# Two attention phases rearranged: transposes one tile later in the second, steps of two key tiles in the first

## The reference

```python
# first attention (layer 0), 16 heads of 16; the last 16 context rows have an attention of their own
q = _ln((x @ Wq + bq).reshape(b, s1, H, HD), qn_w, qn_b)
k = _ln(kv[..., :HD], kn_w, kn_b);  v = kv[..., HD:]        # 1484 rows
s = jnp.einsum('bhqd,bhkd->bhqk', q, k) * SCALE
p = jax.nn.softmax(s, axis=-1)
ctx = jnp.einsum('bhqk,bhkd->bhqd', p, v)
# second attention (layer 1), 16 heads of 128, 1500 rows
q = rmsnorm(q, gq);  k = rmsnorm(k, gk)
scores = jnp.einsum('bqhd,bkhd->bhqk', q, k) * scale
out = jnp.einsum('bhqk,bkhd->bqhd', jax.nn.softmax(scores, axis=-1), v)
```

## Time and profile before

| what | value |
|---|---|
| median of 3 runs | 2623.57 us (2622.91 to 2623.58) |
| the profiled execution, its own time | 2625.33 us |
| its span, first to last instruction | 2623.6 us |
| mean granted TensorE clock | 0.903 of full speed |
| PE busy | 2223.8 us (85%) |
| DVE, ACT, POOL busy | 1781.6, 1187.0, 1236.7 us |
| first attention, first scores to the end of its last products | 913.05 to 1392.5 us |
| second attention, first scores to the last batch's maxima | 1724.17 to 2415.0 us |

### The profile page before, as it was taken

The page is one execution under the profiler, slowest core; times in us unless marked ns, Lnnn a source line. Parts: engine busy times, 40 slices in busy tenths (PEclk is TensorE's granted clock), DMA queues, the critical chain, the costliest instruction groups (busy, mean ns, idle before and its releaser), DMA issues. The chain is left out here.

```text
span 2623.6 us, 47067 instructions
## 1 busy us (share of the span) xinstructions
PE 2223.8 (85%) x16760; PEld 1749.7 (67%) x16760; DVE 1781.6 (68%) x2275; ACT 1187.0 (45%) x2007; POOL 1236.7 (47%) x988
## 2 busy tenths in 40 slices
PE   6999999999954599999996776958898989898675
PEld 4887888787832476666674343448888888888543
DVE  5878888888855465555552336968888888887057
ACT  5888888888820154445451123513232323233202
POOL 5666666666510243333330211318686868687300
PEclk9999999999976599999998687979898989899887
DMA  3232323232213133222220622241121212120500
GB/s 99 111 143 109 142 109 142 109 139 113 120 54 86 69 117 113 103 105 103 103 77 31 205 80 75 86 121 50 50 98 49 98 49 98 49 99 20 208 5 14
DMA packets 93876, 246.16 MB, mean 94 GB/s; under 512 B 19409, under 2 KB 65394, under 8 KB 84450
## 3 DMA queue, kind: packets, MB, share of 16 engines
q1 hardware_dynamic: 87602, 231.17, 24.6%
q10 hardware_dynamic: 4608, 9.44, 0.9%
q0 software_dynamic: 1536, 3.67, 0.5%
HBM read 144.25 MB, written 100.01 MB: 93 GB/s over the span
## 5 line engine op out<-in xcount | busy, mean ns | idle before, releaser
L1150 POOL TENSOR_TENSOR a_S<-a_S,a_mb 128x896 f32<-128x896 f32 x192 | 523.2, 2762 | 218.3 <-ACT a_mb L1173 218.3
L317 DVE TENSOR_REDUCE rk<-n_sq 128x1024 f32 (+2 forms) x384 | 465.6, 1213 | 129.3 <-ACT n_sq L255 126.9
L255 ACT ACTIVATE n_sq<-n_slot 128x1024 f32<-128x1024 f32 (+1 forms) x384 | 394.3, 1027 | 140.3 <-PE n_slot L211 131.8
L994 PEld LDWEIGHTS a_ob<-a_y,a_S 128*128 128x128 f32 (+1 forms) x2688 | 346.8, 203 | 6.9 <-issue 1.9
L994 PE MATMUL a_ob<-a_y,a_S 128*128 128x129 f32 (+1 forms) x2688 | 349.8, 286 | 1.7 <-issue 1.7
L209 PE MATMUL n_slot<-n_wh,n_yh 128*128 128x512 f32 (+1 forms) x768 | 318.3, 414 | 25.1 <-POOL n_yl L153 25.1
L1453 DVE TENSOR_REDUCE a_mpart<-a_pre 112x2 f32<-112x1024 f32 (+1 forms) x192 | 219.1, 1178 | 176.1 <-PE a_pre L1312 176.0
L1398 ACT ACTIVATE a_pr<-a_sc 128x448 f32<-128x448 f32 (+1 forms) x384 | 208.3, 544 | 249.7 <-PE a_sc L1340 238.8
L1179 ACT ACTIVATE a_S<-a_S 128x896 f32<-128x896 f32 x192 | 181.1, 950 | 271.1 <-POOL a_S L1150 270.7
L211 PE MATMUL n_slot<-n_wh,n_yl 128*128 128x512 f32 (+1 forms) x768 | 303.7, 395 | 0.0
L210 PE MATMUL n_slot<-n_wl,n_yh 128*128 128x512 f32 (+1 forms) x768 | 302.0, 393 | 0.0
(11 more groups left out here) (336 smaller groups left out, 4043.6 us busy)
## 6 DMA issues: line engine op xcount, KB each, us to landing
vdram<-n_v SPq DMA_DIRECT2D x16, 1632.0 KB, 5.3
a_v<-vdram SPq DMA_DIRECT2D x16, 1632.0 KB, 6.9
kTdram<-n_kT SPq DMA_DIRECT2D x16, 1484.0 KB, 5.0
a_kT<-kTdram SPq DMA_DIRECT2D x16, 1484.0 KB, 6.5
n_yT<-in_ctxT SPq DMA_DIRECT2D x16, 750.0 KB, 8.9
yhdram<-n_yh SPq DMA_DIRECT2D x16, 750.0 KB, 6.4
yldram<-n_yl SPq DMA_DIRECT2D x16, 750.0 KB, 8.5
a_yh<-yhdram SPq DMA_DIRECT2D x16, 750.0 KB, 6.6
```

The source lines that it names most:

```text
L255: act.activation(sq[0:n, w, :], slot[w][0:n, :], ACT.Square).then_inc(slot_free, 1)
L317: dve.tensor_reduce(g.rk[0:n, b, j, 8 * s:8 * s + 8], sq[0:n, (2 * j + s) % 3, :].rearrange("p (h d) -> p h d", h=8), X, ALU.add)\
L994: mm = pe.matmul(ob[k][:, (q - lo) * (C + 1):(q - lo + 1) * (C + 1)], S[k_][0:n, j, q * P:(q + 1) * P], y1[k_][0:n, j, :], start=(j == 0 a ...
L1150: pool.tensor_tensor(S[1 - i][0:n, j, :], S[1 - i][0:n, j, :], mb[0:n, :], ALU.subtract)\
```

## The change

First attention: PE goes in steps of two key tiles, with the scores of both in a row, then maxima groups in pairs (tables `BETWEEN`, `BEHIND`, `LAST`), then both products. There are three banks `sc`, one bank `ob`, four buffers `pr`. The denominators go into the bank `pre[1]` behind `max_rows` at the end of the step, and POOL's division moves to the next step's begin. PE's program is written out for all steps, without a loop; POOL's loop begins two steps later. Second attention: `maxima`, the reductions and `spread` come one tile later, `mx` has two buffers, and its first entry is a maximum of tiles 0 and 1 in place of a copy.

```diff
-        mx, mb = sb("mx", [P, HQ]), sb("mb", [P, HQ])
+        mx, mb = two("mx", [P, HQ]), sb("mb", [P, HQ])
...
-                        use = 2 * j + half + (2 if j >= 2 else 0)
+                        use = 2 * j + half + (2 if j >= 3 else 0)
...
-                        elif use in (8, 9):
+                        elif use in (10, 11):
                             if from_(b, 1):
-                                pe.wait_ge(mb_ready, 2 * (b - 1) + use - 7)
+                                pe.wait_ge(mb_ready, 2 * (b - 1) + use - 9)
                         else:
-                            pe.wait_ge(s_scaled, SC * b + (use - 4 if use < 8 else use - 6) + 1)
+                            pe.wait_ge(s_scaled, SC * b + (use - 4 if use < 10 else use - 6) + 1)
...
                         if front:
-                            pe.wait_ge(s_scaled, SC * b + half + 1)
-                        r = (USES * i + 4 + half) % RING
+                            pe.wait_ge(s_scaled, SC * b + half + 3)
+                        r = (USES * i + 6 + half) % RING
...
-                    if back and j == 0:
+                    if back and j == 1:
                         maxima(0)
                     if end and j < LAG:
 
                         for t in ((NK - LAG - 1 + j,) if j < LAG - 1 else (NK - 2, NK - 1)):
                             output(b - 2, t, i)
-                    if back and j == 0:
+                    if back and j == 1:
                         maxima(1)
-                    if back and j == 1:
+                    if back and j == 2:
                         spread()
...
+            def reduced(b, k):
+                lo, hi = TI[k]
+                dve.wait_ge(mT_ready, 2 * (b - 1) + k + 1)
+                dve.tensor_reduce(mcol[:, lo:hi], tb[:, 0:(hi - lo) * P].rearrange("p (a n) -> p a n", n=P),
+                                  X, ALU.max).then_inc(mT_taken, 1)
...
-                    if back and j == 0:
-
-                        for k, (lo, hi) in enumerate(TI):
-                            dve.wait_ge(mT_ready, 2 * (b - 1) + k + 1)
-                            dve.tensor_reduce(mcol[:, lo:hi],
-                                              tb[:, 0:(hi - lo) * P].rearrange("p (a n) -> p a n", n=P),
-                                              X, ALU.max).then_inc(mT_taken, 1)
+                    if back and j == 1:
+                        reduced(b, 0)
+                    if front and j == 1:
+                        dve.wait_ge(s_scaled, SC * b + 4)
+                        dve.tensor_tensor(mx[i][:, :], S[i][:, 0, :], S[i][:, 1, :], ALU.max).then_inc(mx_ready, 2)
+                    if back and j == 1:
+                        reduced(b, 1)
                         dve.wait_ge(mT_taken, 2 * b)
                         if from_(b, 2):
                             dve.wait_ge(mb_psum, 2 * (b - 1))
                         dve.tensor_copy(mh[:, :], mcol[:, :]).then_inc(m_high, 1)
                         dve.wait_ge(m_high, b)
                         dve.tensor_tensor(ml[:, :], mcol[:, :], mh[:, :], ALU.subtract).then_inc(m_split, 1)
-                    if front:
-
+                    if front and j >= 2:
                         dve.wait_ge(s_scaled, SC * b + 2 * j + 2)
...
+                        dve.wait_ge(mx_ready, NK * b + j)
+                        dve.tensor_tensor(mx[i][0:n, :], mx[i][0:n, :], S[i][0:n, j, :], ALU.max).then_inc(mx_ready, 1)
...
-    PRE = {1: (0,), 2: (1, 2), 3: (3,), 4: (4, 5), 5: (6,), 6: (7, 8), 7: (9,), 8: (10, 11)}
+    BETWEEN = {6: (6, 7)}
+    BEHIND = {0: (0, 1), 2: (2, 3), 4: (4, 5), 8: (10, 11)}
+    LAST = {6: (8, 9)}
...
-        pr = sb("pr", [P, 3, 2, HALF])
+        pr = sb("pr", [P, 4, 2, HALF])
...
-        sc = [ctx.enter_context(nc.psum_tensor(f"a0_sc{i}", [P, 512], F32)) for i in range(2)]
-        ob = [ctx.enter_context(nc.psum_tensor(f"a0_ob{i}", [P, 512], F32)) for i in range(2)]
+        sc = [ctx.enter_context(nc.psum_tensor(f"a0_sc{i}", [P, 512], F32)) for i in range(3)]
+        ob = ctx.enter_context(nc.psum_tensor("a0_ob", [P, 512], F32))
...
+                if group == 1 and later(b - 2):
+                    pe.wait_ge(rec_ready, b - 2)
...
-                return pr[:, j % 3, h // 8, (h % 8) * NQ:(h % 8 + 1) * NQ]
+                return pr[:, j % 4, h // 8, (h % 8) * NQ:(h % 8 + 1) * NQ]
...
                 if j == 0:
-                    pe.wait_ge(qm_ready, 2 * b + 2)
                     pe.wait_ge(ql_built, 2 * b + 2)
                     pe.wait_ge(k_low, 3 * b + 3)
                 high, low = [m[i][:, :, j * P:j * P + n] for m in (kh, kl)]
                 for half in range(2):
-                    if later(2 * t + half - 1):
-                        pe.wait_ge(p_ready, 2 * t + half - 1)
-                    dst = sc[half][0:n, 0:HALF]
+                    if j == 0:
+                        pe.wait_ge(qm_ready, 2 * b + half + 1)
+                    if later(2 * t + half - 2):
+                        pe.wait_ge(p_ready, 2 * t + half - 2)
+                    dst = sc[(2 * j + half) % 3][0:n, 0:HALF]
...
                 if j == 0:
                     pe.wait_ge(v_in[i], 16 * pair + 16)
-                    if later(b - 1):
-                        pe.wait_ge(rec_ready, b - 1)
+                    if later(b):
+                        pe.wait_ge(o_copied, b)
                 for h in range(H):
                     c, r = h % 4, h // 4
-                    mm = pe.matmul(ob[i][32 * c:32 * c + HD0 + 1, r * NQ:(r + 1) * NQ], v1[i][0:n, j, h, :],
+                    mm = pe.matmul(ob[32 * c:32 * c + HD0 + 1, r * NQ:(r + 1) * NQ], v1[i][0:n, j, h, :],
...
-            def denominators(b, i):
+            def denominators(b):
                 pe.wait_ge(o_copied, b + 1)
-                pe.matmul(ob[i][:, 4 * NQ:8 * NQ], den1[:, :], osum[:, :], start=True, stop=True)\
-                    .then_inc(den_ready, 1)
+                if held(b + 2):
+                    pe.wait_ge(pre_max, 12 * (b + 2) + 12)
+                pe.matmul(pre[1][:, 0, 0:4 * NQ], den1[:, :], osum[:, :], start=True, stop=True).then_inc(den_ready, 1)
...
+            def groups(p, i, which):
+                if held(p + 1):
+                    for group in which:
+                        maxima(p + 1, 1 - i, group)
 
             def step(p, i, pair):
-                for s in range(NK):
+                for s in range(0, NK, 2):
                     if held(p):
                         scores(p, i, s)
+                    groups(p, i, BETWEEN.get(s, ()))
+                    if held(p):
+                        scores(p, i, s + 1)
                     if s == NK - 2 and held(p + 1):
                         max_rows(p + 1)
-                    if held(p + 1):
-                        for group in PRE.get(s, ()):
-                            maxima(p + 1, 1 - i, group)
-                    if s >= PV and held(p):
-                        products(p, i, pair, s - PV)
-                    if s < PV and held(p - 1):
-                        products(p - 1, 1 - i, pair - 1 + i, s - PV + NK)
-                    if s == PV + 1 and held(p - 1):
-                        denominators(p - 1, 1 - i)
-            run(pe, step)
+                    if s == NK - 2 and held(p - 1):
+                        denominators(p - 1)
+                    groups(p, i, BEHIND.get(s, ()))
+                    for j in (s - PV, s - PV + 1):
+                        if s >= PV and held(p):
+                            products(p, i, pair, j)
+                        if s < PV and held(p - 1):
+                            products(p - 1, 1 - i, pair - 1 + i, j + NK)
+                    groups(p, i, LAST.get(s, ()))
+
+            for p in range(-2, B + 1):
+                step(p, p % 2, p // 2)
...
-                            if unit == 0 and later(t - 2):
-                                act.wait_ge(p_used, t - 2)
-                            act.activation(pr[0:n, s % 3, unit, :], sc[unit][0:n, 0:HALF], ACT.Exp).then_inc(p_ready, 1)
+                            if unit == 0 and later(t - 3):
+                                act.wait_ge(p_used, t - 3)
+                            act.activation(pr[0:n, s % 4, unit, :], sc[(2 * s + unit) % 3][0:n, 0:HALF], ACT.Exp).then_inc(p_ready, 1)
...
+            def divide(b):
+                pool.wait_ge(rec_ready, b + 1)
+                by_round = lambda m: m[:, :].rearrange("p (r q) -> p r q", r=4)
...
             def step(p, i, pair):
+                if held(p - 2):
+                    divide(p - 2)
                 for s in range(NK):
                     if s < 3 and held(p + 1):
                         low(p + 1, 1 - i, s)
-                    if s == 5 and held(p - 1):
...
-            run(pool, step)
+            for p in range(-2, 3):
+                step(p, p % 2, p // 2)
+            with pool.Fori(0, B // 2 - 3) as u:
+                step(2 * u + 3, 1, u + 1)
+                step(2 * u + 4, 0, u + 2)
```

(29 more changed lines are left out.)

15 lines of the change are left out of this document (4 added, 11 removed).

## The result

The changed kernel takes 2492.6 us (median of 4 runs, 2491.16 to 2495.5) against 2623.57 (4 runs, 2622.91 to 2625.99): a ratio of 0.950, 95% interval 0.948 to 0.952. That is 131 us less; 113 were forecast. The profiled execution took 2495.5 us.

What follows compares the result with a forecast made beforehand. PE bounds the first attention, plus five jump stops; a batch-boundary chain bounds the second, no engine full. Gains 28 + 25 + 60 = 113 us take the profiled 2625.3 to 2512.3, median 2511 us; range 2492 to 2545.

Steps and rivals of the forecast that it cites:

- The jumps: First attention: PE's five jumps back lose 28.0 us over ten batches, 18.1 of it standing; writing out the program gains it.
- The rival by which the jumps were not the cause: First attention: the five stops remain with PE's program written out; 28 us less gain, 2539 us; chance 5%.
- The slower rival: First attention: written-out program not delivered in time, some 64 blocks at 5.6 us each; 2869 us; chance 2%.
- The steps of two tiles: First attention, PE's order: net gain 1.6 us a batch, 25 us over 16 batches; bounds 0 and 38.
- (a): First attention, PE: 7 score runs a batch in place of 12, at 0.16 us each, gain 0.8 us a batch.
- The new waits: First attention, PE: 0.3 to 0.45 us for `kh`, 0.2 for `dm`, 0.15 for groups 6 and 7; together 0.8 a batch.
- The rival that this part brings nothing: First attention: `kh`, `dm` and the reductions each late by as much again; 25 us lost, 2536 us; chance 8%.
- The transposes: Second attention, transposes one tile later: gain 4.0 us a batch, 15 steps, 60 us; bounds 0 and 90.
- The walk on DVE: Second attention, tile 0's scaling to the output division: 15.5 us in place of 19.55, gain 4.05 a batch.
- The clock: Second attention, batch boundary: PE's clock falls again, costing 16 to 32 us, about 2530 us; chance 22%.

## Why the prediction was right, and where it was off

The direction, the three causes and the places of the new waits held; the size was 18 us short, mainly in two terms. Both ran the same way, and the range held them with 0.6 us to spare, less than the 4.3 us by which the four runs differ. That the time lies inside it is in part luck.

**The jumps** were put at 28.0 us and are worth 26.4 by the run that writes out nothing but them. The undisturbed batch was taken as 28.44, from batch 13; in that run the ten batches from 2 to 12 take 1254.54 - 969.54 = 285.0 us, 28.5 each, which makes the forecast 0.6 too high. The other 1.0 lies within what the medians leave open. The rival by which the jumps were not the cause has fallen, in both directions: without the loop the stops go, with another loop they come back, at the 5.6 us a jump that was forecast. The branch figures of the Trainium skill's page "Advanced Engine Details and Errata", section "Control Flow Timing", are some 51 and 108 ns. The second attention's loop, which fetches no blocks, does not speak against them (half a microsecond for five jumps is less than the medians can tell), and the first's, which has to fetch, does: 5.6 us a jump. The slower rival, blocks not delivered in time, fell with the changed kernel: three blocks in the batch shown, no "issue" stop.

**The steps of two tiles** were put at 1.6 us a batch. Written out alone, the old batches take 28.5 us; the new ones 26.35: 2.15. In the step "(a)" the price of a score run was counted, the price of a switch between two products was not: 0.12 us six times, 0.7 a batch, which is more than the whole miss of 0.55. The products were priced at 0.52 each from a row in which one stood alone. Against it stands the denominators' matmul, put at nothing: at its new place it takes 1282.32 - 1281.79 = 0.53 us, where it took 0.32. The new waits came as listed: 0.44 for `kh` (0.3 to 0.45 forecast), and some 0.2 each before `max_rows` and in the pair between the tiles. The rival that this part brings nothing fell.

**The transposes** were put at 4.0 us a batch and gave 4.51, 69.6 us in all against 60. The walk on DVE erred at its first number: two tiles scaled in a row take 1931.94 - 1929.82 = 2.12 us, not 2 x 1.29 = 2.58. The 1.29, from the scaling of a tile to the reduction behind it, holds a wait: that reduction needs the first transposes, which ran at the low clock and whose record ends at 2018.69 + 1.12 = 2019.81; the reduction starts at 2019.85. In two runs in which these transposes are done before the scaling is, the same pair of instructions is 1.07 and 1.06 apart:

```profile
2016.62 1.14 DVE L1108 TENSOR_TENSOR a_S<-a_ring,rk 128x448 f32<-128x448 f32 x2
2017.69 0.67 DVE L1116 TENSOR_REDUCE a_mcol<-a_tb 128x4 f32<-128x512 f32 x1
```

```profile
2005.31 1.14 DVE L1109 TENSOR_TENSOR a_S<-a_ring,rk 128x448 f32<-128x448 f32 x2
2006.37 0.68 DVE L1117 TENSOR_REDUCE a_mcol<-a_tb 128x4 f32<-128x512 f32 x1
```

Twice that is the 2.12. (The first pair is from the run with the output first, the second from the one with the hole filled.) All behind it is 0.4 earlier: the second transposes at 2.85 us after the boundary and not 3.27, tile 3's scaling at 8.73 and not 9.1, the division at 15.14 and not 15.5. Its waits were forecast as 1.5 us before tile 3 (1.53) and 1.3 on PE before the second transposes (0.50, with 0.90 before the scores and 0.90 before the first transposes). The 0.8 less comes from both sides: DVE's reduction is 0.4 earlier, and PE's output ends at 2.35 and not at 2.0, since its record reaches 1.73 us from its start and not the 1.48 that lie between two starts. **The clock** was the likeliest rival, at 22%. It did not come true: PE's three stops of 0.90, 0.90 and 0.50 left the granted clock at 1.00. The run with a stop of 1.01 and one of 2.22 shows that it could have. That a half of this part's gain comes with the clock alone follows only from the run with the hole filled; the prediction had the mechanism, but no price for it by itself.

Outside the two attentions nothing moved by more than the 1.7 us of the tail, as assumed. The sum: 26.4 for the jumps, 68.4 for the transposes and, as what is left of 131, 36 for the steps of two tiles (16 batches by 2.15 are 34), against 28, 60 and 25.

## What to carry to other kernels

When an operation is moved next to another of its own kind, price it from a row in which two stand in a row, not from one that stands alone: the products were priced too high for this. When a price is the distance of two starts, look whether the second instruction had to wait for another engine: the scaling's 1.29 us held such a wait, too short to be listed as idle time. When a stop is followed by work at the low clock, its price is read from the distances of batch begins, with the stop and without it, not as the length of the stop. And before an operation is put into a hole of an engine, look at what stands behind it: the output moved alone shortened the hole and gained nothing, since the clock still fell and the same wait came back one tile later.

## What the runs showed of the hardware

- A jump back cost PE 3.7 us of standing and 1.9 more behind it, with a stretch at the low clock, where the loop's code had to be fetched again, and nothing that could be measured in a loop for which the trace shows no fetched block. In each of nine such stops the only packet moved was one instruction block of 16 KB.
- Sixteen useless matmuls in a hole of 3.8 us, at the boundaries of one phase, made the kernel 31 us faster; the granted clock there was 1.00 in place of 0.50.
- Three stops of PE of 0.90, 0.90 and 0.50 us, with work between, left the clock at full speed; behind stops of 1.01 and 2.22 us it fell. A stop as long as the 3.78 us of the earlier trace rows is not needed for the clock to fall.
- 64 small matmuls into four column groups took 0.92 us where two times 32, apart, took 0.52 each.
- Two scalings of 128x448 on DVE take 1.06 us before two more of their kind (2.12 for four), and 1.06 to 1.07 before a reduction whose input is ready. Before a maximum that reads their result it is 1.27 to 1.30 (1925.25 - 1923.98 and 1935.92 - 1934.62 in the changed kernel).
